# Writing out the last turn of a cross-attention and routing kernel: six tiles routed after the last row maximum

## The reference, cut to what matters

```
x = x + tanh(g_xattn[0]) * attention(layernorm(x), ctx)      # 16 heads of 16, softmax over 375 keys, then @ Wo + bo
t = layernorm(x).reshape(896, 256);  probs = softmax(t @ wg);  idx = argmax(probs)
locations = cumsum(one_hot(idx)) - one_hot(idx)              # place of a token within its expert, in token order
keep a token if its place < 112;  gate = probs at idx (0 if not kept)
x = x + tanh(g_ffn[0]) * gate * (t @ W[idx].T + b[idx])
```

## Time and profile before

| what | us |
| --- | --- |
| three timed runs | 213.04, 215.04, 216.35 |
| their median | 215.04 |
| span of the profiled execution, first to last instruction | 212.4 |
| PE busy in that span | 180.8 |
| DVE busy | 138.6 |
| ACT busy | 80.8 |
| POOL busy | 78.3 |

### The profile page before, as it was taken

The page is one execution under the profiler, slowest core; times in us unless marked ns, Lnnn a source line. Parts: engine busy times, 40 slices in busy tenths (PEclk is TensorE's granted clock), DMA queues, the critical chain, the costliest instruction groups (busy, mean ns, idle before and its releaser), DMA issues.

```text
span 212.4 us, 4545 instructions
## 1 busy us (share of the span) xinstructions
PE 180.8 (85%) x1754; PEld 132.9 (63%) x1754; DVE 138.6 (65%) x325; ACT 80.8 (38%) x174; POOL 78.3 (37%) x96
## 2 busy tenths in 40 slices
PE   0899879288994999999999999898687859689993
PEld 0567535155782788788788787676375655448751
DVE  6124897982876588588588588649759612566463
ACT  2213323211671268268258258551273513112100
POOL 7302998560056002982601601600602550004640
PEclk9999969976997999999999999999999969999999
DMA  5946376672000844672664670569310526610201
GB/s 181 249 109 158 91 157 178 141 196 56 0 3 1 205 97 147 145 210 86 133 168 142 144 216 27 134 193 303 101 40 1 173 71 163 189 37 9 82 27 40
DMA packets 26477, 25.51 MB, mean 120 GB/s; under 512 B 9613, under 2 KB 24857, under 8 KB 26456
## 3 DMA queue, kind: packets, MB, share of 16 engines
q1 hardware_dynamic: 24754, 22.60, 40.7%
q0 software_dynamic: 864, 2.07, 3.2%
q10 hardware_dynamic: 838, 0.55, 0.8%
HBM read 8.36 MB, written 5.06 MB: 63 GB/s over the span
## 4 chain that ended last, share of the span: by engine, by line
PE 74%; DVE 16%; DMA 3%; issue 2%; ACT 2%; POOL 0%; SPq 0%; DVEq 0%; POOLq 0%
PE pj L436 12%; PE pv L514 10%; PE sT L499 9%; PE sc L471 9%; PE pj L457 9%; DVE nmax L955 5%; PE sc L695 4%; PE misc L528 4%; DMA ctx_sb<-in_ctxT 3%; PE pj L679 3%; PE pj L445 3%; DVE xn L918 2%; PE sc L457 2%; PE sT L695 2%; DVE mparts L962 1%
## 5 line engine op out<-in xcount | busy, mean ns | idle before, releaser
L955 DVE TENSOR_REDUCE nmax<-sc 112x1 f32<-112x375 f32 x128 | 67.1, 542 | 28.3 <-PE sc L471 25.7
L793 ACT ACTIVATE prob<-sT 125x448 f32<-125x448 f32 x96 | 49.9, 544 | 60.0 <-PE sT L499 59.6
L471 PE MATMUL sc<-k,q 126*112 126x375 bf16 x128 | 41.5, 342 | 9.8 <-DVE nmax L955 9.1
L499 PEld LDWEIGHTS sT<-q,k 128*125 128x125 bf16 x384 | 32.1, 139 | 8.0 <-issue 3.1
L1226 POOL TENSOR_SCALAR ve<-mv 112x1 f32<-112x1 f32 (+2 forms) x11 | 2.7, 249 | 91.2 <-DVE mv L1024 78.4
L499 PE MATMUL sT<-q,k 128*125 128x112 bf16 x384 | 35.0, 225 | 0.9 <-ACT prob L793 0.7
L436 PE MATMUL pj<-ctx_sb,wk_sb 128*128 128x375 f32 x64 | 29.3, 592 | 6.8 <-DMA ctx_sb<-in_ctxT 6.8
L471 PEld LDWEIGHTS sc<-k,q 126*112 126x112 bf16 x128 | 16.4, 132 | 18.9 <-DVE nmax L955 15.2
L457 PE MATMUL pj<-wv_sb,ctx_sb 128*125 128x256 f32 x84 | 23.2, 408 | 0.0
L514 PE MATMUL pv<-prob,v_sb 125*32 125x112 f32 x768 | 22.7, 269 | 0.0
L436 PEld LDWEIGHTS pj<-ctx_sb,wk_sb 128*128 128x128 f32 x64 | 14.3, 233 | 13.2 <-issue 8.4
(11 more groups left out here) (148 smaller groups left out, 243.2 us busy)
## 6 DMA issues: line engine op xcount, KB each, us to landing
k<-parts_k SPq DMA_DIRECT2D x42, 187.5 KB, 2.9
q<-parts_q SPq DMA_DIRECT2D x45, 56.0 KB, 2.4
ctx_sb<-in_ctxT SPq DMA_DIRECT2D x8, 281.2 KB, 3.8
wT_sb<-in_wT SPq DMA_DIRECT2D x8, 256.0 KB, 3.1
slots<-xin SPq DMA_DIRECT2D x1, 1799.0 KB, 8.2
k<-parts_k SPq DMA_DIRECT2D x12, 93.8 KB, 2.3
xin<-slots SPq DMA_DIRECT2D x8, 112.9 KB, 2.2
xin<-slots SPq DMA_DIRECT2D x8, 112.0 KB, 2.2
```

Of the source, the lines that this page charges most:

```text
L471: pe.matmul(sc[i % 2][0:NQ, 0:NK], q6[0:MAXROW, b % RING, h, :], k6[0:MAXROW, b % RING, h, :], start=True, stop=True).then_inc(s_sc, 1)
L499: mm = pe.matmul(st[n % 2][0:CK, j * NQ:(j + 1) * NQ], k6[:, b % RING, h, c * CK:(c + 1) * CK], q6[:, b % RING, h, :], start=True, stop=True)
L793: nc.scalar.activation(prob[0:CK, n, :], st[n % 2][0:CK, 0:4 * NQ], ACT.Exp, scale=SCALE).then_inc(s_p, 1)
L955: nc.vector.tensor_reduce(nmax[:, h:h + 1], sc[i % 2][0:NQ, 0:NK], axis=AX.X, op=ALU.max, negate=True).then_inc(s_max, 1)
```

## The change

The loops over turns stop ahead of turn 7 on PE, ACT and DVE, and that turn is written out as a plain list on each. The instructions are the same in number and shape; their order is not.

- DVE takes eight maxima, splits them, takes six more, scales the heads of batch 6, takes the last two and splits; adds x for tile 6 and takes its statistics; only then comes `top_expert(0)`, then `normalise_2(6)`, `gates(0)` and `assign(0)`. Behind that, `normalise_heads(7)`, the addition of x and `normalise_2(7)` move in between the combines of tile 6, and routing of tile 7 moves ahead of most results.
- PE spreads the turned units of batch 6 over the scores of batch 7; `places(0)` moves behind the logits of tile 6; the second V product of batch 7 moves ahead of `dense(0, 2)`, `through_wo(7)` ahead of `dense(0, 3)`, `turn_xn2(7)` and `logits(7)` ahead of or beside the first expert, `dense(1, 0)` and `dense(1, 1)` between experts 0 to 3.
- ACT follows PE's order; `router_exp(2)` comes behind four experts, where it was last.
- POOL takes the inverse root of tile 6 first and then sends all six tiles in one go.

```diff
 PE   -            for t in range(B):
      +            for t in range(LAST):
...
+            last_scores(12, 13)
+            turned(LAST, 0, 1)
+            last_scores(13, 14)
...
+            through_wo(LAST - 1)
+            turn_last_max(1)
+            turned(LAST, 5, 6)
...
+            half_of_probs_v(LAST, 0)
+            turn_xn2(LAST - 1)
+            turned(LAST, HALF, HALF + 2)
+            logits(LAST - 1)
+            pe.wait_ge(s_tri, 2)
+            places(0)
+            turned(LAST, HALF + 2, HALF + 4)
...
             dense(0, 0)
+            turned(LAST, HALF + 4, UNITS)
             dense(0, 1)
             places(1)
+            half_of_probs_v(LAST, 1)
             dense(0, 2)
+            pe.wait_ge(s_mix, 1)
+            through_wo(LAST)
             dense(0, 3)
+            turn_xn2(LAST)
             turn_expert(0)
+            logits(LAST)
+            dense(1, 0)
             turn_expert(1)
             product(0)
             turn_expert(2)
             product(1)
+            dense(1, 1)
             turn_expert(3)
+            places(2)
             product(2)
 ACT
+            exps(LAST, HALF, UNITS)
+            router_exp(1)
+            leave_x2T(LAST)
+            for e in range(4):
                 leave_expert(e)
             router_exp(2)
+            for e in range(4, E):
+                leave_expert(e)
 DVE
+            last_maxima(0, 8)
+            split_last_max(0)
+            last_maxima(8, 14)
+            normalise_heads(LAST - 1)
+            last_maxima(14, 16)
+            split_last_max(1)
+            add_x(LAST - 1)
+            sums_2(LAST - 1)
+            variance_2(LAST - 1)
...
+            top_expert(0)
             normalise_2(LAST - 1)
+            gates(0)
+            assign(0)
...
             top_expert(2)
+            result(0)
             gates(2)
             result(1)
             weigh(2)
 POOL
+            pool.wait_ge(s_stat2, LAST)
+            rstd(ve2, mv2, rs2, LAST - 1, LAST).then_inc(s_rstd2, 1)
             pool.wait_ge(s_cleared, 16)
             pool.wait_ge(s_slot, 1)
-            scatter(0, 4)
-            pool.wait_ge(s_stat2, LAST)
-            rstd(ve2, mv2, rs2, LAST - 1, LAST).then_inc(s_rstd2, 1)
-            scatter(4, 6)
+            scatter(0, 6)
```

More of the change, by code:

```diff
@@ L575, in _ @@
             pe.wait_ge(s_ve, 2)
-            for t in range(B):
+            for t in range(LAST):
                 if t == 1:
@@ L636, in _ @@
                         logits(t - 3)
-                    if t < LAST and n == MAX_AT:
+                    if n == MAX_AT:
                         turn_max(t)
@@ L643, in _, with last_scores @@
                         if n == LATE_WO_AT:
[L644 to L647, removed]
+                            pe.wait_ge(s_mrows, t + 1)
                             through_wo(t - 1)
[L649 to L659, removed]
+            def last_scores(lo, hi):
+                for i in range(lo, hi):
+                    scores(LAST, i)
@@ new lines, in turned @@
+            def turned(b, lo, hi):
+                for u in range(lo, hi):
+                    scores_T(b, u)
+            last_scores(0, 2)
+            turned(LAST - 1, 0, 2)
+            last_scores(2, 3)
+            pe.wait_ge(s_x1, LAST - 1)
+            turn_xn2(LAST - 3)
+            turned(LAST - 1, 2, 4)
+            last_scores(3, 4)
+            turned(LAST - 1, 4, 5)
+            last_scores(4, 5)
+            turned(LAST - 1, 5, 6)
+            last_scores(5, 6)
+            logits(LAST - 3)
@@ new lines, in _ @@
+            turn_xn2(LAST - 2)
+            turned(LAST - 1, 6, 7)
+            last_scores(6, 7)
+            turned(LAST - 1, 7, 8)
+            last_scores(7, 8)
+            logits(LAST - 2)
+            turned(LAST - 1, 8, 9)
+            half_of_probs_v(LAST - 1, 0)
+            turned(LAST - 1, 9, 10)
+            last_scores(8, 9)
+            turn_last_max(0)
+            turned(LAST - 1, 10, 11)
+            last_scores(9, 10)
+            turned(LAST - 1, 11, 12)
+            last_scores(10, 12)
@@ L737, in _ @@
             turn_expert(7)
-            dense(1, 0)
-            places(2)
             product(6)
-            dense(1, 1)
             product(7)
@@ L866, in _ @@
                         leave_x2T(t - 3)
[L867 to L874, removed]
                     if t + 1 < B:
@@ L883, in leave_expert, with exps @@
                 leave(xinT[e].rearrange("p c n -> p (c n)"), sc[e % 2][:, 0:2 * CAP], s_xinTe)
-            leave_x2T(LAST - 1)
[L886 to L890, removed]
+            def exps(b, lo, hi):
+                for u in range(lo, hi):
+                    probs(b, u)
+            exps(LAST - 1, 0, 2)
+            leave_x2T(LAST - 3)
+            exps(LAST - 1, 2, 6)
+            leave_x2T(LAST - 2)
+            exps(LAST - 1, 6, 10)
+            leave_last_max(0)
+            exps(LAST - 1, 10, UNITS)
+            exps(LAST, 0, 5)
+            leave_last_max(1)
+            exps(LAST, 5, HALF)
+            router_exp(0)
+            leave_x2T(LAST - 1)
+            exps(LAST, HALF, UNITS)
+            router_exp(1)
+            leave_x2T(LAST)
+            for e in range(4):
                 leave_expert(e)
[L892 to L895, removed]
             router_exp(2)
+            for e in range(4, E):
+                leave_expert(e)
         @block.vector
@@ L1147, in _ @@
                             turn_back(t - 1)
[L1148 to L1159, removed]
+                    if n == SPLIT_AT:
                         split_max(t)
-                    if n == MAX_AT and t < LAST:
+                    if n == MAX_AT:
                         leave_max_rows(t)
@@ L1186, in combine, with last_maxima @@
                     so_far, ALU.mult, ALU.add).then_inc(s_read, 1)
+            def last_maxima(lo, hi):
+                for i in range(lo, hi):
+                    take_max(LAST, i)
+            last_maxima(0, 8)
[7 more added lines that the diff above has]
+            variance_2(LAST - 1)
+            dve.wait_ge(s_eno, 1)
+            dve.wait_ge(s_token, 1)
+            top_expert(0)
             normalise_2(LAST - 1)
+            gates(0)
+            assign(0)
             top_expert(1)
@@ L1191, in _ @@
             weigh(1)
-            for e in range(6):
-                combine(0, e)
+            combine(0, 0)
+            combine(0, 1)
             normalise_heads(LAST)
-            combine(0, 6)
-            combine(0, 7)
-            result(0)
+            combine(0, 2)
+            combine(0, 3)
             add_x(LAST)
@@ L1200, in _ @@
             variance_2(LAST)
-            result(1)
[L1202 to L1206, removed]
+            combine(0, 4)
+            combine(0, 5)
+            normalise_2(LAST)
+            combine(0, 6)
+            combine(0, 7)
+            top_expert(2)
+            result(0)
+            gates(2)
+            result(1)
             weigh(2)
-            result(5)
-            result(6)
             combine(1, 0)
             combine(1, 1)
-            result(7)
-            for e in range(2, E):
+            result(2)
+            combine(1, 2)
+            combine(1, 3)
+            for e in range(3, E):
+                result(e)
+            for e in range(4, E):
                 combine(1, e)
```

31 lines of the change are left out of this document (6 added, 25 removed).

## The result

The changed kernel takes 207.06 us (median of 4 runs, 203.51 to 209.20), the kernel before 214.04 in the same set of runs (4 runs, 212.92 to 216.35): ratio 0.9535, 95% interval 0.9426 to 0.9644. In a second set it was 207.51 against 214.79, 0.9606 (0.9527 to 0.9685). These ratios leave out runs over 1.5% above the fastest of their kernel. The forecast was 213.2 in 210.9 to 216.2: the direction is right, the gain (7.0 and 7.3 us by the two pairs of medians) about four times the 1.8 that was forecast.

The account below looks back on a forecast made before the run. PE was taken to bound the end by when it enters the expert stage and its waits there: first turning 2.4 us sooner, stage 0.5 longer, so -1.9 on the span and 213.2 us, range 210.9 to 216.2.

Parts of the forecast that it names:

- costs about 1.6 us: Behind PE's 2.79 us wait for tile 6: half-clock work from 172.2 to 176.0 costs about 1.6 us, which the change removes.
- I take 2.95: Small copies of the two spare rows with the maxima: 2.95 us from issue to use, read as at most 3.04.
- the wait that was forecast at the first turned unit of batch 7: PE in turn 7, behind the second V half: stands 0.8 us until the first copy of maxima lands at 163.2.
- Case 3 of the rivals: Small copies land in 1.8 us, moving all 0.95 forward, and waits uncover no weight loads, 0.7 more: 211.5 us; chance 0.13.
- The expert stage: First expert's turning to last combine: 22.0 us, 0.5 longer, as products 3, 4, 5 wait 0.4, 1.1, 0.2 plus weight loads.
- The routing chain: From the end of `assign` through POOL's six serial writes to SP's load of the first expert: 10.5 us, its earlier cover spent.
- the tie that was forecast: At the first expert's turning: PE's own order (186.2) and the arrival of the expert's rows (186.1) come together.
- the blocking of which the Trainium skill speaks: DVE instructions with two SBUF inputs and POOL's writes block each other; 0.24 us more per write would end 0.6 later.
- case 2: Expert rows land later than 186.1 and decide the end, so the kernel is slower: 215.9 us; chance 0.12.
- Case 1: Low clock returns behind the remaining waits of 1.2 and 0.2 us near tile 6: 214.7 us; chance 0.27 together with rival 4.

Follow-up runs that it names:

- before_filled: Kernel before plus three matmuls with unused results on PE in the wait ahead of turning tile 6; 0.9871 of the kernel before, late part 58.03 us.
- v_half_behind: Changed kernel with the first V half of batch 7 put back behind the turning of tile 6; 0.9764 of the kernel before, late part 57.30 us.
- copy_twice: Changed kernel with each of the two small copies of the last maxima made in two steps via a spare tile; one run, 209.75 us.
- route_7_first: Changed kernel with the routing of tile 7 moved ahead of the expert results on PE, ACT and DVE; 206.68 us, 0.9666 of the kernel before.

## Why the prediction was wrong

**The low clock was priced from one execution.** The first step that failed is "costs about 1.6 us". The mechanism at the wait was read rightly: the clock is low behind the wait at tile 6, the change closes the wait, and before_filled and v_half_behind show it from both sides. But the way from tile 6 to the first expert, 15.04 us at 2.4 GHz (before_filled), took 1.4 us more in the first profile (16.42) and 4.2 in the two others (19.26, 19.27). And the forecast knew nothing of a second place, the low clock inside turn 7, which cost nothing in the first profile and 1.4 us in both others; the new order of turn 7 never showed it. The mean of the three late parts (59.49, 63.66, 63.68) is 62.3 against 58.0, so the clock is worth 4.2 us on the average of these three, where the forecast had 1.6. The Trainium skill (TensorE: Matmul & The Clock Gate, What's actually happening) says that PE's recent activity sets the clock; these runs agree, with 1.00 where the wait was filled and 0.77 where it was not. Why the low clock comes in one execution and not in another, and lasts so differently, stays open.

**The small copies were priced from a row that did not show them.** The second step that failed is "I take 2.95". It rested on the turned unit at 152.70, which stood behind a score matmul that itself had waited for DVE: an upper bound, taken as the value though the nearest row, the last store, had 1.8. The changed kernel shows 1.99 (143.87 to 145.86), copy_twice 1.80. Counted from the first score (150.6 in the forecast, 144.85 in the trace), the first eight maxima were forecast to end at 7.4 us and end at 6.30; the fourteenth maximum 13.7 and 12.35; x added 17.0 and 15.27; tile 6 turned 19.9 and **18.04**. About 1.1 of the 1.9 is there at the eighth maximum, behind the first copy. The other 0.8 is as much as the wait that was forecast at the first turned unit of batch 7 and did not come; that this is all of it is argued from the order, no run changes the time of a copy downwards. Case 3 of the rivals named the copies, and put 0.95 us on them.

**The expert stage was to be 0.5 longer and is 0.3 shorter**, 21.2 against 21.48, so 0.8 off. The place was right: DVE stands 3.23 us for the exp of tile 7, products 3 and 4 wait. The sizes were not: 0.17, 0.91 and nothing for product 5, instead of 0.4, 1.1 and 0.2, with a weight load added to each. route_7_first shows that the chain named there was the one: without it the stage is 1.8 us shorter.

**Right by its steps.** The routing chain: from the end of `assign` to the load 10.63 us (165.59 to 176.22), forecast 10.5; its cover is spent as said, since PE turned tile 7 at 177.78 and the first expert's turning at 178.27 was released by the load, the tie that was forecast. The writes took 0.94 to 1.20 us (0.94 to 1.19 before), the last started 6.52 behind the first (6.49 forecast): the blocking of which the Trainium skill speaks (SBUF — State Buffer, Who interferes with whom) is not seen in them. So case 2 did not come. Case 1 did not either, in three profiles of the changed kernel.

**The sum.** Order at 2.4 GHz, 58.0 - 54.6 = 3.4 (forecast 0.3 by the same steps); clock 4.2 (forecast 1.6); together 7.7 (62.3 - 54.6), where the two pairs of medians differ by 7.0 and 7.3. Of the 3.1 us that the order was priced too low, 1.9 lie up to the turning of tile 6, 0.3 up to the first expert (15.38 us; 186.2 - 170.5 = 15.7 in the forecast) and 0.8 to 0.9 in the expert stage. So the direction came from the right mechanism, but the larger part of the gain from terms that were mis-sized. The early part adds to each execution a few microseconds either way, and in the first pair of profiles 5.8.

## What to carry to other kernels

A wait on PE has two prices, its length and the clock behind it; the second differs between executions of the same program, so it is read from several profiles, or taken away with filler matmuls to get the yardstick at full clock. Compare profiles by stretches that begin at a named instruction, since the span mixes the change with what happened ahead of it. And the time that a transfer takes is only read from a row where the transfer itself ended the wait.

## What the runs showed of the hardware

The same 2.79 us wait was followed by about 3 us at 1.2 GHz in one execution and by about 9 in two others, with the same instructions behind it. Turn 7 in the old order, up to tile 6 and with a wait of 1.41 us there, ran at a granted clock of 0.92 in one execution and of 1.00 in another. Why stays open. The early part of the program, instruction for instruction the same, took 144.85 to 151.00 us; in the first profile of before the matmuls at 12.75 us still ran at about half speed (2.87 for four) where those of the changed kernel at 11.40 did not (1.53), though the page shows the clock as full in that slice: up to the first change of clock on record the durations have to be read instead. A copy of 7 KB between tiles takes 1.99 us from issue to use, one of 3.5 KB 1.80.
